# Asking for a weight piece before the factors of unit 0

## The chip, the cores and the metric

One core of one Trainium2 chip runs the kernel. The metric is the device time of one execution in microseconds (us), as the median over several executions. An engine's name stands for its queue of instructions: PE is the matrix engine (TensorE), PEld its weight loads, DVE VectorE, ACT ScalarE, POOL GpSimd, and SP (SyncE) only issues DMAs and waits. ACT issues a few DMAs too.

## What is computed

The reference is a compressed interaction network of three layers over x of shape (512, 39, 32), with 39 fields and 32 embedding columns:

```python
for i in range(3):
    z = einsum('bmd,bnd->bmnd', x, hidden).reshape(B, -1, D)
    cur = relu(einsum('bcd,co->bod', z, Ws[i]) + bs[i][None, :, None])
    # layers 0 and 1: the first 100 of 200 outputs are the next hidden, the rest are kept
    # layer 2: all 200 are kept
result = concatenate(kept, axis=1).sum(axis=-1)      # (512, 400)
```

Everything is float32. Layer 0 has 39 x 39 pairs (780 different ones), layers 1 and 2 have 39 x 100 pairs.

## The kernel before

**Units.** The batch is cut into 4 tiles of 128 rows, and for each tile the 32 columns d are worked one after the other. A pair (tile, d) is a unit, and there are 128 units. For a unit the DVE multiplies two factors into products z (pairs on the partitions, batch rows along the free dimension), ACT rounds z to z_high, DVE makes z_low = z - z_high, and PE multiplies both with weights that are split in the same way (`w_split`, high and low half side by side). That is a float32 product by fast matmuls.

**x by unit.** The factors are rows of x turned round. PE transposes x (`turn_x`, L939), ACT copies the result to SBUF (L770), and `store_x` (L298) writes it with 8 DMAs (L304, L306) to a DRAM tensor `x_by_unit`. From there `load_pairs(u)` (L309) fetches the two factors of layer 0 of unit u, `x_left` and `x_right`, with 6 DMAs over 39 partitions each (L312, L313). `load_xb_rest` (L323) fetches x rows for layers 1 and 2 into the last 32 partitions of `xb`. For units 0 and 1 the other 96 partitions of `xb` are made on PE (L952) and copied by ACT and DVE.

**Weights.** Layer 0's weights fold the two halves of the symmetric pair matrix. They come in by `load_w0` (near part from SP, far part from ACT's queue, both into the memory of z) and are summed on DVE (L587, semaphore `pair_sum`). Layers 1 and 2 have 31 chunks each, loaded in four pieces: `load_w(queue, l, g, ...)` (L251) fetches piece g of layer l into one of two places of a staging area in `mixed` (L260 for 96 partitions, L262 for 32 partitions; a full piece is 600 KB and 200 KB). ACT rounds it into `w_split` (`high_piece`, L774), then DVE writes the low half (`low_piece`, L494). The next piece for the same place waits for that.

**Order.** Each engine has its own program written by hand, and semaphores join them. All places of this case lie in the first 90 us of the program. On SP the order is: load x; copy W0 twice into DRAM (L338, L340); near part of layer 0's weights; `store_x(0)`; wait until all 8 stores have landed (`xt_done`); `load_pairs(0)`; piece 0 of layer 1's weights; wait for the repeats on PE (`repeated`); piece 1; wait for DVE's first product; `load_pairs(1)`; `load_xb_rest` of unit 0; and so on. On DVE: `pair_sum` (L587), `product0` of unit 0 (L514), low half of layer 0's weights, z_low, `low_piece(1, 1, 0)`, `sums`, `low_piece(2, 1, 1)`, `product0` of unit 1, then the first product of layer 1 (L541). On ACT: high half of layer 0's weights, two repeats, z_high, two more repeats, `high_piece(1, 0)`, `second_half` (L731, reads PE's result of unit 0), `dup` (L741), `high_piece(1, 1)`. On PE: repeats, layer 0 of unit 0, a transpose, layer 0 of unit 1, then layers 1 and 0 by turns.

Piece 0 is staged in columns 0 to 1599 of `mixed`; the tile of x that is being turned and stored lies in its last 1280 columns (of 4224), and piece 1 overlaps that.

Of the kernel before, what the change touches and what calls it, by code (L numbers as in the profile page):

```python
# [74 lines left out]
def split_from(layer, g):  # L75
    return WHOLE if (layer, g) == (2, 0) else 0


def split_chunks(layer, g):
    return group_chunks(g) - split_from(layer, g)  # L80
# [23 lines left out]
def cin_kernel(nc, r_x, W0, W1, W2, b0, b1, b2, out):  # L104
# [6 lines left out]
    with ExitStack() as ctx:  # L111
# [90 lines left out]
        def stage(l, g):  # L202
            at, n = g % 2 * STAGED, split_chunks(l, g)
            return mixed[:, at:at + n * O].rearrange("p (c o) -> p c o", o=O)
# [10 lines left out]
        def xts(r):  # L215
            return x_tile(r).rearrange("p (k t) -> p k t", t=T)
# [34 lines left out]
        def load_w(queue, l, g, w, bias):  # L251
            k = GROUPS * (l - 1) + g
            skip, n = split_from(l, g), split_chunks(l, g)
            a = GROUP * g + skip
            wt, row = w.tensor, HID * O
            st = stage(l, g)
            if skip:
                queue.dma_start(w_whole[0:MAIN, :, :], bass.AP(wt, 0, [[O, MAIN], [row, skip], [1, O]])).then_inc(w_whole_in, 16)
                queue.dma_start(w_whole[MAIN:P, :, :], bass.AP(wt, CHUNKS * row, [[O, P - MAIN], [row, skip], [1, O]])).then_inc(w_whole_in, 16)
            queue.dma_start(st[0:MAIN, :, :], bass.AP(wt, a * row, [[O, MAIN], [row, n], [1, O]])).then_inc(w_in[k], 16)  # L260
            if g < GROUPS - 1:
                queue.dma_start(st[MAIN:P, :, :],  # L262
                                bass.AP(wt, (CHUNKS + skip) * row + 32 * g * O, [[O, P - MAIN], [row, n], [1, O]])).then_inc(w_in[k], 16)
            else:
                queue.wait_ge(stage_ready, l)
                full = F // TAIL_CHUNKS
                at = MAIN + TAIL * full
                for t in range(TAIL):
                    queue.dma_start(st[MAIN + t:at:TAIL, 0:TAIL_CHUNKS, :],
                                    bass.AP(wt, (MAIN + t) * O, [[TAIL_CHUNKS * row, full], [row, TAIL_CHUNKS], [1, O]])).then_inc(w_in[k], 16)  # L270
                queue.dma_start(st[at:at + TAIL, 0:F - TAIL_CHUNKS * full, :],
                                bass.AP(wt, TAIL_CHUNKS * full * row + MAIN * O, [[O, TAIL], [row, F - TAIL_CHUNKS * full], [1, O]]))\
                     .then_inc(w_in[k], 16)
                queue.dma_start(st[ONES_ROW:ONES_ROW + 1, 0, :], bass.AP(bias.tensor, 0, [[O, 1], [1, O]])).then_inc(w_in[k], 16)
# [16 lines left out]
        def _(sp):  # L291
# [6 lines left out]
            def store_x(r):  # L298

                sp.wait_ge(xts_in, X_BANKS * (r + 1))  # L300
                at = r * (D * XROWS * T)
                for q in range(Q):
                    part = xts(r)[D * q:D * (q + 1), :, :]
                    sp.dma_start(bass.AP(xt_t, at + q * T, [[XROWS * T, D], [Q * T, BLOCKS], [1, T]]), part).then_inc(xt_done, 16)  # L304
                    k = 1 if q == 0 else 0
                    sp.dma_start(bass.AP(xt_t, at + (F + Q * k + q) * T, [[XROWS * T, D], [Q * T, WRAP_BLOCKS - k], [1, T]]),  # L306
                                 part[:, k:WRAP_BLOCKS, :]).then_inc(xt_done, 16)
# [35 lines left out]
            load_w0(sp, True)  # L343
            sp.dma_start(pair_w[L0_ONES:L0_ROWS, 0, :], bass.AP(b0.tensor, 0, [[O, 1], [1, O]])).then_inc(pairs_w_in, 16)
            store_x(0)
            sp.wait_ge(xt_done, 16 * X_STORES)
            sp.wait_ge(ones_l0, 2)
            load_pairs(0)
            sp.wait_ge(ones_set, 2)
            load_w(sp, 1, 0, W1, b1)  # L350

            sp.wait_ge(repeated, 2 * HALVES * Q)
            load_w(sp, 1, 1, W1, b1)
# [694 lines left out]
```

## Time and profile before

| | us |
|---|---|
| median of 3 executions | 2685.38 |
| lowest, highest | 2685.25, 2686.32 |
| the profiled execution, its time | 2686.64 |
| the profiled execution, its span from first to last instruction | 2684.8 |
| PE busy in the span | 2652.3 (99%) |
| DVE busy | 2633.4 (98%) |
| ACT busy | 1782.6 (66%) |
| DMA, mean over the span | 133 GB/s |

The span is 1.84 us shorter than the time of the same execution; what lies around it is start and end. Times in the trace count from the span's start. Engine queues that only issue carry a q (SPq). In a timeline row the bracket tells how long the engine sat idle before the instruction and what released it. KB are 1024 bytes, MB are 10^6 bytes.

### The profile page before, as it was taken

How to read it: one execution, taken by the hardware profiler on the slowest of the kernel's cores; microseconds unless marked ns; L12 is line 12 of the kernel's file. 1: busy time of each engine (PE TensorE's matmuls, PEld its weight loads, DVE VectorE, ACT ScalarE, POOL GpSimd, SP SyncE). 2: the span in 40 equal slices, each digit the busy share in tenths (PEclk: the TensorE clock that was granted, in tenths of full speed). 3: DMA queues.
4: the chain of work that ended last, by engine and by line, in shares of the span. 5: the costliest groups of instructions: out<-in, count | busy, mean ns of one | idle time of the engine just before them, and what ended most of it. 6: DMA issues, size and time to landing. Idle time of an engine off the chain costs nothing.

```text
span 2684.8 us, 53056 instructions
## 1 busy us (share of the span) xinstructions
PE 2652.3 (99%) x17992; PEld 2639.2 (98%) x17992; DVE 2633.4 (98%) x2593; ACT 1782.6 (66%) x2978; POOL 121.4 (5%) x148
## 2 busy tenths in 40 slices
PE   6999999999999999999999999999999999999999
PEld 4999999999999999999999999999999999999998
DVE  6999999999999999999999999999999999999998
ACT  4666666666666666666666666666666666666665
POOL 0000000000000000000000000000000000000000
PEclk8999999999999999999999999999999999999999
DMA  8555545545565555455456544554555455455542
GB/s 187 138 143 142 132 121 138 141 121 125 143 156 128 129 142 130 120 137 140 125 138 152 140 120 127 143 131 120 135 144 127 124 141 137 120 128 143 129 120 72
DMA packets 249154, 357.76 MB, mean 133 GB/s; under 512 B 30631, under 2 KB 184019, under 8 KB 248959
## 3 DMA queue, kind: packets, MB, share of 16 engines
q1 hardware_dynamic: 229091, 330.02, 47.1%
q0 software_dynamic: 18960, 25.76, 5.5%
q8 instruction: 54, 0.88, 0.1%
q10 hardware_dynamic: 1008, 0.75, 0.1%
q14 instruction: 41, 0.34, 0.0%
HBM read 325.98 MB, written 5.91 MB: 124 GB/s over the span
## 4 chain that ended last, share of the span: by engine, by line
PE 97%; DVE 1%; issue 1%; SPq 1%; DMA 1%; ACT 0%; DVEq 0%
PE acc L917 64%; PE acc L918 30%; PE acc L910 2%; PE turned L930 1%; DVE z_low L547 0%; DMA xb<-x_by_unit 0%; DVE z L541 0%; DMA x_by_unit<-mixed 0%; DMA x_right<-x_by_unit 0%; PE x_turned L939 0%; SPq L338 0%; ACT w_split L774 0%; SPq L340 0%; SPq L312 0%; DVE z L514 0%
## 5 line engine op out<-in xcount | busy, mean ns | idle before, releaser
L917 PE MATMUL acc<-w_split,z_high 128*128 128x400 f32 (+1 forms) x8704 | 2602.7, 367 | 20.4 <-DVE z_low L547 16.4
L918 PE MATMUL acc<-w_split,z_low 128*128 128x200 f32 (+1 forms) x8704 | 2221.8, 255 | 0.0
L726 ACT ACTIVATE z_high<-z 128x1024 fp32r<-128x1024 f32 (+2 forms) x1152 | 1165.7, 1012 | 798.1 <-PE acc L918 497.9
L918 PEld LDWEIGHTS acc<-w_split,z_low 128*128 128x128 f32 (+1 forms) x8704 | 1664.7, 191 | 0.0
L917 PEld LDWEIGHTS acc<-w_split,z_high 128*128 128x128 f32 (+1 forms) x8704 | 1637.3, 188 | 23.6 <-issue 16.1
L547 DVE TENSOR_TENSOR z_low<-z,z_high 128x1024 fp32r<-128x1024 f32 (+2 forms) x1152 | 1336.6, 1160 | 19.1 <-ACT z_high L726 6.9
L541 DVE TENSOR_TENSOR z<-mixed,xb 128x1024 f32<-128x1024 f32 (+1 forms) x1024 | 1213.2, 1185 | 1.1 <-DMA xb<-x_by_unit 0.9
L446 POOL DMA_DIRECT2D direct<-fresh_direct x129 | 113.5, 879 | 2327.6 <-ACT fresh_direct L765 2306.8
L751 ACT ACTIVATE mixed<-turned 32x128 f32<-32x128 f32 x768 | 205.4, 267 | 8.9
L748 ACT ACTIVATE mixed<-turned 96x512 f32<-96x512 f32 x256 | 150.9, 590 | 6.0 <-PE turned L930 1.9
L514 DVE TENSOR_TENSOR z<-x_left,x_right 118x896 f32<-118x896 f32 x128 | 138.6, 1083 | 3.3 <-DMA x_right<-x_by_unit 3.3
L557 DVE TENSOR_TENSOR s<-acc,half 128x400 f32<-128x400 f32 (+1 forms) x130 | 73.0, 562 | 0.7 <-ACT half L731 0.7
L749 ACT ACTIVATE mixed<-turned 32x128 f32<-32x128 f32 x256 | 69.3, 271 | 3.0
L731 ACT ACTIVATE half<-acc 128x400 f32<-128x400 f32 (+1 forms) x130 | 65.0, 500 | 7.6 <-PE acc L918 4.6
L765 ACT ACTIVATE fresh_direct<-s 128x400 f32<-128x400 f32 x126 | 68.0, 539 | 3.1
L910 PE MATMUL acc<-w_whole,z 128*128 128x200 f32 x256 | 66.5, 342 | 0.8 <-DVE s L566 0.8
L741 ACT ACTIVATE s<-s 128x48 f32<-128x48 f32 (+1 forms) x130 | 31.4, 241 | 45.5 <-DVE s L557 45.5
L566 DVE TENSOR_TENSOR s<-acc,half 128x200 f32<-128x200 f32 x128 | 46.0, 360 | 5.7 <-issue 4.0
L930 PE MATMUL turned<-s 128*128 128x128 f32 x256 | 49.3, 273 | 1.1 <-ACT s L741 1.1
L736 ACT ACTIVATE half<-acc 128x200 f32<-128x200 f32 x128 | 40.8, 318 | 7.8 <-PE acc L918 7.8
L910 PEld LDWEIGHTS acc<-w_whole,z 128*128 128x128 f32 x256 | 38.3, 189 | 1.1 <-DVE s L566 1.1
L930 PEld LDWEIGHTS turned<-s 128*128 128x128 f32 x256 | 29.9, 140 | 1.5 <-ACT s L741 1.5
(30 smaller groups left out, 96.7 us busy)
## 6 DMA issues: line engine op xcount, KB each, us to landing
xb<-x_by_unit SPq DMA_DIRECT2D x378, 384.0 KB, 5.2
x_right<-x_by_unit SPq DMA_DIRECT2D x384, 136.5 KB
xb<-x_by_unit SPq DMA_DIRECT2D x384, 128.0 KB, 5.9
xb<-x_by_unit SPq DMA_DIRECT2D x126, 336.0 KB
direct<-fresh_direct POOLq DMA_DIRECT2D x115, 200.0 KB, 7.1
xb<-x_by_unit SPq DMA_DIRECT2D x128, 84.0 KB
x_left<-x_by_unit SPq DMA_DIRECT2D x384, 19.5 KB
mixed<-in_L_rec_W_dram SPq DMA_DIRECT2D x5, 600.0 KB, 6.7
```

What stands on the lines that cost most here:

```text
L446: return pool.dma_start(direct[:, a:b, :].rearrange("p l o -> p (l o)"), fresh_direct[:, a:b, :].rearrange("p l o -> p (l o)"), accum_op=A ...
L514: nc.vector.tensor_tensor(dst, left, x_right[0:L0_ROWS, :, :], ALU.mult).then_inc(product, 1)
L541: nc.vector.tensor_tensor(dst, left, xb[par][:, c0:c0 + n, :], ALU.mult).then_inc(product, 1)
L547: nc.vector.tensor_tensor(z_low[slot % LOW_RING][0:rows, 0:n * T], z[0:rows, z_place(number, slot), 0:n * T], z_high[slot % RING][0:rows, ...
L557: nc.vector.tensor_tensor(s[:, a:b, :, 0:HID], acc[:, a:b, 0:O].rearrange("p l (h o) -> p l h o", o=HID), half[:, a:b, :, :], ALU.add).the ...
L726: nc.scalar.activation(z_high[slot % RING][0:rows, 0:n * T], z[0:rows, z_place(number, slot), 0:n * T], ACT.Copy).then_inc(high, 1)
L748: nc.scalar.activation(h[0:MAIN, :, :], t[0:MAIN, :].unsqueeze(1).to_broadcast([MAIN, GROUPS, T]), ACT.Relu)
L751: last = nc.scalar.activation(h[MAIN:P, g, :], t[32 * g:32 * (g + 1), :], ACT.Relu)
L910: used = nc.tensor.matmul(a[:, 0:O], z_whole[:, c * T:(c + 1) * T], w_whole[:, c, :], start=(c == 0), stop=False, skip_group_check=True)
L917: nc.tensor.matmul(a[:, 0:2 * O], z_high[slot % RING][0:rows, tok], w, start=(c == 0), stop=False, skip_group_check=True)
L918: last = nc.tensor.matmul(a[:, 0:O], z_low[slot % LOW_RING][0:rows, tok], w[:, 0:O], start=False, stop=(c == chunks - 1), skip_group_check ...
L930: last = nc.tensor.transpose(turned[:, 0, l * P:(l + 1) * P], s[:, l, 0, :], ident)
```

## The change

The call that asks for piece 0 of layer 1's weights is moved up on SP: from behind `load_pairs(0)` and the wait for `ones_set` to directly behind `store_x(0)`, ahead of the wait for the stores' landing. The wait for `ones_set` then stands in front of piece 1. Nothing else moves; the other engines' programs are the same.

```diff
             store_x(0)
+            load_w(sp, 1, 0, W1, b1)
             sp.wait_ge(xt_done, 16 * X_STORES)
             sp.wait_ge(ones_l0, 2)
             load_pairs(0)
             sp.wait_ge(ones_set, 2)
-            load_w(sp, 1, 0, W1, b1)
 
             sp.wait_ge(repeated, 2 * HALVES * Q)
             load_w(sp, 1, 1, W1, b1)
```

On SP's queue, from the end of `store_x(0)` (L304, L306) to the first DMA of `load_pairs(1)` (the last row). `mixed<-in_L_rec_W_dram` with 96x8x200 and 32x8x200 is one piece of layer 1's weights; the difference between before (-) and the change (+), with the semaphores waited for:

```order
 L304 DMA x_by_unit<-mixed 32x10x128
 L306 DMA x_by_unit<-mixed 32x5x128
+L260 DMA mixed<-in_L_rec_W_dram 96x8x200
+L262 DMA mixed<-in_L_rec_W_dram 32x8x200
 L312 DMA x_left<-x_by_unit 39x128 [waits ones_l0,xt_done]
 L313 DMA x_right<-x_by_unit 39x7x128
```

The two DMAs of piece 0 now stand between the last store and the wait that `load_pairs(0)` begins with. And where they were:

```order
 L312 DMA x_left<-x_by_unit 39x128
 L313 DMA x_right<-x_by_unit 39x7x128
-L260 DMA mixed<-in_L_rec_W_dram 96x8x200 [waits ones_set]
-L262 DMA mixed<-in_L_rec_W_dram 32x8x200
-L260 DMA mixed<-in_L_rec_W_dram 96x8x200 [waits repeated]
+L260 DMA mixed<-in_L_rec_W_dram 96x8x200 [waits repeated,ones_set]
 L262 DMA mixed<-in_L_rec_W_dram 32x8x200
 L312 DMA x_left<-x_by_unit 39x128 [waits product]
```

Here only piece 1 is left between `load_pairs(0)` and `load_pairs(1)`.

## Rows read from the trace of the kernel before

**Rows 1.** The page: PE's line of busy time, and the chain by engine

```profile
PE 2652.3 (99%) x17992; PEld 2639.2 (98%) x17992; DVE 2633.4 (98%) x2593; ACT 1782.6 (66%) x2978; POOL 121.4 (5%) x148
PE 97%; DVE 1%; issue 1%; SPq 1%; DMA 1%; ACT 0%; DVEq 0%
```

**Rows 2.** Waits of DVE, 20 to 90 us: waited for, us in total, times, longest

```profile
DVE w_split L494 <- ACT w_split L774: 6.0, 5, 2.3
```

**Rows 3.** Waits of PE, 41 to 90 us, same columns

```profile
PE acc L917 <- DVE s L557: 3.2, 1, 3.2
```

**Rows 4.** The chain in order of time, 14 to 42 us: start, us, what

```profile
14.74 4.23 DMA x_by_unit<-mixed
...
21.09 3.62 DMA x_right<-x_by_unit
...
28.75 9.24 DMA xb<-x_by_unit
```

**Rows 5.** Timeline of SP, 14 to 25 us: start, us, engine, line, DMA

```profile
14.74 0.57 SPq L306 DMA_DIRECT2D x_by_unit<-mixed  x1
18.98 0.34 SPq L312 DMA_DIRECT2D x_left<-x_by_unit  x1
...
21.51 0.40 SPq L260 DMA_DIRECT2D mixed<-in_L_rec_W_dram  x1
21.95 0.54 SPq L262 DMA_DIRECT2D mixed<-in_L_rec_W_dram  x1
24.03 0.31 SPq L260 DMA_DIRECT2D mixed<-in_L_rec_W_dram  x1
```

**Rows 6.** Four stretches; the last three columns are PEclk, DMA share, GB/s

```profile
17.25:19.00 1.75, 1.75 (x6) 0.69 (x5) 0.55 (x1) 0.75 (x2) 0.00 (x0) 1.00 0.83 231
19.00:21.00 2.00, 2.00 (x6) 0.71 (x5) 0.87 (x2) 0.78 (x2) 0.00 (x0) 1.00 0.47 99
21.00:23.25 2.25, 2.25 (x7) 0.87 (x6) 1.44 (x1) 1.78 (x3) 0.00 (x0) 1.00 0.68 170
...
25.00:27.00 2.00, 0.00 (x0) 0.00 (x0) 2.00 (x2) 1.00 (x2) 0.00 (x0) 1.00 1.12 239
```

**Rows 7.** The page of 23 to 25 us: GB/s in 40 slices of 0.05 us

```profile
GB/s 143 152 117 80 32 32 64 128 208 192 176 223 196 228 180 244 196 196 228 224 240 208 304 192 272 240 288 208 352 304 304 272 272 208 240 208 240 224 304 256
```

**Rows 8.** DMA queues (q1 SP, q10 ACT), 17.25 to 19, then 19 to 21 us

```profile
q10 hardware_dynamic: 456, 0.34, 70.1%
q1 hardware_dynamic: 141, 0.06, 12.8%
...
q10 hardware_dynamic: 126, 0.09, 28.9%
q1 hardware_dynamic: 227, 0.11, 18.6%
```

**Rows 9.** Timelines of DVE, ACT and PE, 20 to 38 us, by engine

```profile
20.82 1.62 DVE L587 TENSOR_TENSOR z<-z 118x1400 f32<-118x1400 f32 x1 [1.03 <-DMA z<-w_rows_again]
24.82 1.09 DVE L514 TENSOR_TENSOR z<-x_left,x_right 118x896 f32<-118x896 f32 x1 [2.38 <-DMA x_right<-x_by_unit]
...
34.95 1.83 DVE L494 TENSOR_TENSOR w_split<-mixed,w_split 128x1600 fp32r<-128x1600 f32 x1 [1.53 <-ACT w_split L774]
37.66 1.09 DVE L514 TENSOR_TENSOR z<-x_left,x_right 118x896 f32<-118x896 f32 x1 [0.89 <-DMA x_right<-x_by_unit]
...
29.16 1.54 ACT L774 ACTIVATE w_split<-mixed 128x1600 fp32r<-128x1600 f32 x1 [1.34 <-DMA mixed<-in_L_rec_W_dram]
32.44 0.34 ACT L731 ACTIVATE half<-acc 128x200 f32<-128x200 f32 x1 [1.74 <-PE acc L918]
...
33.40 1.52 ACT L774 ACTIVATE w_split<-mixed 128x1600 fp32r<-128x1600 f32 x1
...
28.58 0.42 PE L917 MATMUL acc<-w_split,z_high 118*128 118x400 f32 x1 [4.58 <-DVE z_low L547]
```

**Rows 10.** The microsecond in which PE's first multiplication ends, columns as rows 6

```profile
32.00:33.00 1.00, 0.40 (x2) 0.03 (x1) 0.74 (x2) 0.34 (x1) 0.00 (x0) 0.83 1.10 152
```

## The prediction, made before the change was run

> **What bounds the kernel now.** I read the page first: PE is busy 99% of the span and holds 97% of the chain that ended last [rows 1]. So from about 85 us on the time is PE's own work, the change does not touch it, and all that the change can do is to move the moment at which that work gets going. The waits before it tell who sets that moment. The longest wait of PE for DVE's sums ends at 62.85 us [rows 3], and DVE itself waits in 20 to 90 us mainly for ACT's rounded weights, 6.0 us in five waits [rows 2], and for two landings of `x_right`, 2.38 us and 0.89 us [rows 9]. From 38.7 us on DVE's timeline has no more idle time than three gaps of 0.7 to 0.8 us behind ACT, each of which hangs on work that DVE or PE gave out shortly before. A shift of DVE's start at 37.66 us therefore goes through to the end, one to one. The question is what the change does to the instruction at 37.66 us, `product0` of unit 1.
>
> Three transfers lie in the chain on the way there [rows 4]: the last store of x (4.23 us), `x_right` of unit 0 (3.62 us from its issue at 21.09), and the rest of `xb` (9.24 us from its issue at 28.75, landed at 37.99).
>
> **The change, part by part.**
>
> *Issue on SP.* Two DMAs of piece 0, 0.40 and 0.54 us [rows 5], about 0.95 us with the gaps, now stand behind the last store, whose issue ends at 15.31. SP then waits anyway until 18.98 for the stores' landing, 3.67 us. The 0.95 us are hidden there; if that cover were gone they would cost 0.95 us. `load_pairs(0)` is still issued from 18.98 on. Piece 1 is issued at 24.03 behind the wait for PE's repeats [rows 5]; `load_pairs(0)` was issued by 21.46, so removing 0.95 us behind it moves nothing. The moved wait for `ones_set` costs nothing: DVE's two fills of `xb` are over by 7 us. Piece 0 is requested at 15.35 instead of 21.51, 6.2 us earlier.
>
> *What is released earlier.* ACT waits 1.34 us for piece 0, until 29.16 [rows 9]. Taken alone that wait goes. What is late next? ACT's next step but one, `second_half`, waits for PE's result until 32.44 (1.74 us idle), and the next weights, at 33.40, come only after it [rows 9]. So the 1.34 us are worth nothing to the path: piece 0's low half is on DVE earlier, and PE doesn't need it before 45 us.
>
> *What the DMA queue gains later.* At 37.66 DVE had been idle for 0.89 us behind `low_piece` of piece 1 (34.95, ended 36.77), until `x_right` of unit 1 landed [rows 9]. The following product of layer 1 starts at 38.67, 0.68 us after `xb` landed. Between 25 and 38 us the DMA engines are full (1.12 at 25 to 27 [rows 6]), and most of piece 0, 0.82 MB, stands in that queue ahead of piece 1, the factors of unit 1 and the rest of `xb`. With it gone, 2 to 3 us of this backlog go, and less than one is needed. So `product0` of unit 1 starts at 36.77 instead of 37.66: **0.89 us gained**, and no more, since DVE is busy with `low_piece` up to there.
>
> *What unit 0's factors lose.* This is the term that decides. Piece 0 is now in SP's own DMA queue ahead of the six loads of `load_pairs(0)`. Its bytes take 0.82 MB / 239 GB/s = 3.43 us at the rate of 25 to 27 us, when mostly such weights move [rows 6]. They start about 1.8 us behind the issue: piece 0, issued at 21.51 before, began to move at about 23.3, where the rate climbs again after a dip to 32 GB/s that ends the factors [rows 7]. So now they start at about 17.2, and up to 23.25, where the last bytes of unit 0's factors moved before, they compete with the far part of layer 0's weights (ACT's queue, q10) and the factors. How much room is there? By the share of all 16 engines the idle part is 1.75 x (1 - 0.83) + 2.00 x (1 - 0.47) + 2.25 x (1 - 0.68) = 0.30 + 1.06 + 0.72 = 2.1 us [rows 6]. By that the factors are 3.4 - 2.1 = 1.3 us late. But q10 keeps a share of only 0.70 from 17.25 to 19 although 126 more of its packets are still to come [rows 8], so I read that it uses only about 0.7 to 0.75 of the engines, and these are full: 0.70 / 0.75 + 0.13 is over 1. On them the room is 0 in the first stretch, 2.00 x (1 - 0.289 / 0.75 - 0.186) = 0.86 us in the second, and 0.72 us in the third [rows 6, 8], 1.6 us in all. A transfer lands when its last engine is done, so I take this: 3.43 - 1.58 = **1.9 us late**. The bounds: 0 (the room is used wholly and the packets overlap better than in any stretch shown) and 3.4 us (none of it is used, since the requests stand in a strict order). It can't be below 0: nothing makes the factors of unit 0 earlier.
>
> The Trainium skill (DMA: Bandwidth & Descriptors, "Why a DMA increments its semaphore by 16 and not by 1") has a rule for this: a DMA runs on the largest number of engines, up to 16, that divides its outer dimensions. By it the far weights (24 rows) sit on 12 engines and the factors (39 rows) on 13. The room on the busiest engines would then be some 1.1 us and the factors 2.3 us late, and the sum below would end 0.4 us higher.
>
> *Does the pair sum become the bound?* The far weights landed at 20.8 and their sum ended at 22.44 [rows 9], 2.38 us ahead of the product. Piece 0 shares the engines with them from 17.25 on; even the whole 3.43 us give a landing at 24.2 and an end at 25.9. With the factors landing at 24.8 + 1.9 = 26.7 this stays hidden, and so does ACT's rounding of layer 0's weights (1.4 us), which DVE needs one product later.
>
> *The way from there.* `product0` of unit 0 (24.82) is followed by z_high, z_low, PE's first multiplication at 28.58, `second_half` at 32.44, the sums, and ACT's rounding of piece 1 at 33.40, then DVE's `low_piece` at 34.95 [rows 9]. Each waits for the one before it, so `low_piece` ends 1.9 us later, at 38.7. The same product also releases `load_pairs(1)` and the rest of `xb` on SP, which are issued 1.9 us later: `xb` from 30.7 on. Landing had taken 9.24 us with the queue full; now there are 2 us or more less in it, so it lands by about 37, and DVE needs it at 39.7. PE's clock was at half (1.2 GHz) during that multiplication, after 4.58 us of idleness before it [rows 9], and rose again in 32 to 33 us, where the mean granted was 0.83 [rows 10]. It starts even later now, so it runs at half speed again; if the rise came at the same 32.4 us as before, its last 1.9 us would take half as long, a gain of up to 1 us. I keep this for the range.
>
> **The sum.** +1.9 (factors of unit 0 late) - 0.9 (wait at 37.66 gone) = +1.0 us. On the profiled execution: 2686.64 + 1.0 = 2687.6. The median of the runs, 2685.38, is 1.26 us below that execution, so for a median **2686.4 us**. That is 0.04% slower. A measurement of this kernel can tell about 0.2%, 5.4 us, from no change, so it will count as the same.
>
> **The rivals.**
>
> *A. There is room, and the early request pays.* If piece 0 slips into the idle DMA time before the factors, these are under 0.9 us late and the kernel gets faster, by 0.9 us at the most: 2684.5 to 2685.4. For it: 0.47 share and 99 GB/s at 19 to 21 us [rows 6]. Against it: this dip is short, and piece 0 needs 3.4 us. The Trainium skill (DMA: Bandwidth & Descriptors, "Rules for kernel authors") says for this, in my words, to issue a DMA early and to wait for it late so that its fixed cost is overlapped. Followed as written, it gives this rival.
>
> *B. The factors stand strictly behind the whole piece, and the stores are held up too.* Piece 0 is asked for while stores are still landing (4.23 us for the last [rows 4], in a full DMA). If it takes bandwidth from them, SP is released after 18.98, and with no room used the factors land 3.4 us late and up to 1 us more. Price: +2.5 to +3.5 us, 2687.9 to 2688.9. It decides from the point at which the factors are over 0.9 us late; under that the waits at 37.66 cover it. To get beyond 0.2% they would have to be over 6.3 us late, nearly twice piece 0's whole transfer.
>
> *C. The shift is absorbed.* Between 38 and 85 us something else, such as PE's clock rising earlier or DVE's gaps behind ACT, takes up the microsecond: 2685.1 to 2685.7. PE has idle time there, 3.2 us before 62.85 alone [rows 3], but it isn't the one that is late. DVE is, and it has hardly a gap.
>
> **How the numbers follow.** My forecast (factors 0.9 to 3.0 us late, +0 to +2.1 us) gets 0.60, A 0.17, B 0.13, C 0.10. The range reaches from A's end, 2684.5, to +2.9 or so, 2688.3, and 0.4 us on each side for the scatter of a median whose runs lie 1.07 us apart: 2684.1 to 2688.7. All four lie within 0.2% (2680.0 to 2690.8); 0.01 for faster and 0.02 for slower are for mechanisms that I don't see.
>
> **What would show it.** In the profile after: the weight DMAs at about 15.3 and 15.8 on SP, and `load_pairs(0)` still at about 19.0 (else B). DVE's wait for `x_right` before its first product about 1.9 us longer, that product at 26.7 (A: under 25.7; B: over 28). ACT's wait of 1.34 us for piece 0 gone. DVE's wait at 37.66 gone, with `product0` of unit 1 directly behind `low_piece` at about 38.7. DMA full from 15 to about 25 us and then a dip, until piece 1 starts to move at about 25.8. The span 1 us longer. The prediction would be wrong if the factors land at the old time, if `product0` of unit 1 still waits for a DMA, or if the shift at 38 us isn't the shift at 85 us.

## The result and the profile after

The changed kernel takes 2690.59 us (median of 20 runs, 2689.29 to 2692.12). The kernel before, run 20 times beside it, takes 2686.24 us. The ratio is 1.0015, with a 95% interval of 1.0009 to 1.0021: it is slower by 0.15%, 4.35 us. That is under the 0.2% that I had set as the bound of "the same", but clear of noise, and four times the 1.0 us that I had forecast. The range ended at 2688.7.

The profiled execution took 2690.58 us with a span of 2688.8 us, 4.0 us more than before. Its page begins as before's does [rows 1]:

```profile
PE 2655.2 (99%) x17992; PEld 2642.1 (98%) x17992; DVE 2632.8 (98%) x2593; ACT 1782.2 (66%) x2978; POOL 121.4 (5%) x148
PE 97%; DVE 1%; issue 1%; SPq 1%; DMA 0%; ACT 0%; DVEq 0%; ACTq 0%
```

PE is 2.9 us longer busy at the same number of instructions, so it ran more of them at the lower clock than before. The timeline of SP (start, us, engine, line, DMA), to be read beside [rows 5]:

```profile
14.71 0.48 SPq L306 DMA_DIRECT2D x_by_unit<-mixed  x1
15.24 0.86 SPq L260 DMA_DIRECT2D mixed<-in_L_rec_W_dram  x1
16.14 0.75 SPq L262 DMA_DIRECT2D mixed<-in_L_rec_W_dram  x1
18.65 0.32 SPq L312 DMA_DIRECT2D x_left<-x_by_unit  x1
```

The piece is asked for at 15.24, and the wait for the stores ends at 18.65, no later than before. The rest is told by DVE and ACT, to be read beside [rows 9]:

```profile
26.10 1.62 DVE L587 TENSOR_TENSOR z<-z 118x1400 f32<-118x1400 f32 x1 [5.62 <-DMA z<-w_rows_again]
28.12 1.09 DVE L514 TENSOR_TENSOR z<-x_left,x_right 118x896 f32<-118x896 f32 x1 [0.41 <-DMA x_right<-x_by_unit]
...
38.59 1.83 DVE L494 TENSOR_TENSOR w_split<-mixed,w_split 128x1600 fp32r<-128x1600 f32 x1 [1.53 <-ACT w_split L774]
40.33 1.08 DVE L514 TENSOR_TENSOR z<-x_left,x_right 118x896 f32<-118x896 f32 x1
...
31.19 1.54 ACT L774 ACTIVATE w_split<-mixed 128x1600 fp32r<-128x1600 f32 x1
36.08 0.34 ACT L731 ACTIVATE half<-acc 128x200 f32<-128x200 f32 x1 [3.35 <-PE acc L918]
...
31.92 0.67 PE L917 MATMUL acc<-w_split,z_high 118*128 118x400 f32 x1 [7.23 <-DVE z_low L547]
```

Two things had got late. `product0` of unit 0 starts at 28.12 and not 24.82, 3.3 us later. And the sum of layer 0's weights (L587) starts at 26.10 and not 20.82, 5.3 us later: it ends only 0.4 us ahead of the factors' landing. Both waits that I had expected to vanish have vanished: ACT no longer waits for piece 0 (31.19), and `product0` of unit 1 follows `low_piece` at once (40.33). So the table of shifts reads:

| instruction | before, us | after, us | shift |
|---|---|---|---|
| `product0` of unit 0 on DVE | 24.82 | 28.12 | +3.30 |
| PE's first multiplication | 28.58 | 31.92 | +3.34 |
| `second_half` on ACT | 32.44 | 36.08 | +3.64 |
| `low_piece` of piece 1 on DVE | 34.95 | 38.59 | +3.64 |
| `product0` of unit 1 on DVE | 37.66 | 40.33 | +2.67 |
| last `low_piece` on DVE | 81.70 | 84.31 | +2.61 |
| PE's x transposes of tile 1 (chain) | 133.79 | 136.37 | +2.58 |
| a z_low in the last unit (chain) | 2670.98 | 2673.56 | +2.58 |
| end of the span | 2684.8 | 2688.8 | +4.0 |

Between 134 us and the last unit, a stretch of over 2500 us, not a hundredth of a microsecond is added or lost. The remaining 1.4 us come behind 2673 us. Here are the stretches around PE's last wait, first of the kernel before, then of the changed one (the third number from the right is the granted clock):

```profile
2669.00:2673.00 4.00, 1.65 (x9) 1.18 (x8) 3.43 (x4) 2.23 (x3) 0.00 (x0) 1.00 0.01 4
2673.00:2677.00 4.00, 4.00 (x27) 3.79 (x27) 4.00 (x5) 2.02 (x2) 0.00 (x0) 1.00 0.00 2
```

```profile
2671.00:2675.00 4.00, 1.65 (x10) 1.09 (x9) 2.85 (x4) 2.23 (x3) 0.00 (x0) 1.00 0.02 4
2675.00:2679.00 4.00, 4.00 (x19) 3.98 (x18) 4.00 (x4) 2.01 (x2) 0.00 (x0) 0.59 0.00 2
```

PE is busy for 1.65 us of the first four in both, but in the changed kernel's execution the clock then fell to 1.2 GHz for most of the next four microseconds, and PE got 19 matmuls done and not 27. Whether that belongs to the change is what some of the experiments are for.

### The profile page after: what moved, and what is told of

Read it like the earlier page. It is cut to its first block, busy times and chain, and to the rows that moved or that the text cites. A ratio compares the mean times of both kernels' runs of the same rounds, so it can differ in the third digit from the quotient of the medians.

```text
span 2688.8 us, 53057 instructions
## 1 busy us (share of the span) xinstructions
PE 2655.2 (99%) x17992; PEld 2642.1 (98%) x17992; DVE 2632.8 (98%) x2593; ACT 1782.2 (66%) x2978; POOL 121.4 (5%) x148
## 4 chain that ended last, share of the span: by engine, by line
PE 97%; DVE 1%; issue 1%; SPq 1%; DMA 0%; ACT 0%; DVEq 0%; ACTq 0%
PE acc L917 64%; PE acc L918 30%; PE acc L910 2%; PE turned L930 1%; DVE z_low L547 0%; DVE z L541 0%; DMA x_right<-x_by_unit 0%; DMA x_by_unit<-mixed 0%; PE x_turned L939 0%; DVE z L514 0%; SPq L338 0%; ACT w_split L774 0%; SPq L340 0%; DVE w_split L494 0%; SPq L304 0%
## 5 line engine op out<-in xcount | busy, mean ns | idle before, releaser
L514 DVE TENSOR_TENSOR z<-x_left,x_right 118x896 f32<-118x896 f32 x128 | 138.2, 1079 | 0.4 <-DMA x_right<-x_by_unit 0.4
```

The source lines that it names most:

```text
L514: nc.vector.tensor_tensor(dst, left, x_right[0:L0_ROWS, :, :], ALU.mult).then_inc(product, 1)
```

## The experiments

All the theories here are about three questions: what makes the factors of unit 0 late and why by 3.3 us and not by 1.9; whether PE's clock has a part in the start; and whether the drop of the clock at the end belongs to the change. Ratios are to runs of the kernel before on the same chip; "product0" is the start of L514 of unit 0 on DVE.

**Both kernels a second time** (before_again, after_again).

> The kernel before, unchanged, for a second trace. Theory start (the whole difference is made before 90 us by unit 0's factors being late): product0 of unit 0 starts at 24.8 and DVE's product at 83.2 again, and the last part has no waits that differ. Theory end (1.3 to 1.5 us of the difference come from PE's clock dropping for one step close to the end, by chance of phase): in this second trace the end can show such a drop too, and then its span is about 1.4 us longer than 2684.8 with the same start.

> The changed kernel, unchanged, for a second trace. Both theories: product0 of unit 0 at about 28.1 (3.3 us late), DVE at 85 us shifted by about 2.6 us. Theory start: ratio to before 1.0015 made by that alone, about 4 us, each time. Theory end: the end either shows the 3.4 us drop of the clock again (span 2688.8) or not (span 2687.4).

Before: 2687.18 us (2684.99 to 2688.39, 11 runs), ratio 1.0 (0.9991 to 1.0009), product0 at 25.19, span 2686.6. Changed: 2690.27 us (2688.63 to 2692.17, 11 runs), ratio 1.0011 (1.0002 to 1.002), product0 at 28.03, span 2688.9. The lateness of the factors and of the weight sum repeats:

```profile
25.33 1.62 DVE L587 TENSOR_TENSOR z<-z 118x1400 f32<-118x1400 f32 x1 [4.75 <-DMA z<-w_rows_again]
28.03 1.09 DVE L514 TENSOR_TENSOR z<-x_left,x_right 118x896 f32<-118x896 f32 x1 [1.08 <-DMA x_right<-x_by_unit]
```

The rest varies. In the second trace of before, DVE waited 0.66 us at `product0` of unit 1 (38.11), and its last `low_piece` came at 83.08, 1.4 us later than in the first trace. The shift of that instruction is 2.6 us between the first two traces and only 0.7 us between the second two (83.76 in the changed kernel). A single pair of traces does not give the shift to a microsecond. The drop of the clock at the end is there again in the changed kernel and again not in the kernel before.

**Less of the piece, and more** (small_early, more_early). First only the part for 32 partitions is asked for early, and the part for 96 at the old place:

```diff
             store_x(0)
-            load_w(sp, 1, 0, W1, b1)
+            load_w(sp, 1, 0, W1, b1, "small")
...
             sp.wait_ge(ones_set, 2)
+            load_w(sp, 1, 0, W1, b1, "large")
```

> Only the 32-partition part of piece 0 (200 KB of 800) is asked for ahead of the factors, the 600 KB part stays at the old place. Theory order (the factors are late by the time that the bytes ahead of them in SP's queue take): factors 0.8 us late, a quarter of 3.3, product0 of unit 0 at 25.6, wait at 37.66 partly gone, total about that of before. Rival room (there is idle DMA time at 19 to 21 us that takes a small request): factors 0 to 0.3 us late, product0 of unit 0 at 24.8 to 25.1.

```profile
22.78 1.62 DVE L591 TENSOR_TENSOR z<-z 118x1400 f32<-118x1400 f32 x1 [2.93 <-DMA z<-w_rows_again]
25.53 1.09 DVE L518 TENSOR_TENSOR z<-x_left,x_right 118x896 f32<-118x896 f32 x1 [1.14 <-DMA x_right<-x_by_unit]
```

(Lines of this kernel are 4 higher.) product0 at 25.53, 0.7 us later than in the mean of three traces of before, 24.85 (24.82, 25.19 and, below, 24.53). 2688.16 us (11 runs), ratio 1.0006 (0.9997 to 1.0015), so the total is not told from before's. That looks as if even 200 KB, which need 0.9 us of the DMA, found no room. But SP's timeline tells where the 0.7 us arose:

```profile
19.75 0.34 SPq L315 DMA_DIRECT2D x_left<-x_by_unit  x1
```

The stores released SP at 19.75, and not at 18.98, 19.03 and 18.74 as in those three traces. From there product0 followed after 5.78 us, against 5.84, 6.16 and 5.79. So behind the release the 200 KB cost nothing; the 0.7 us are the later landing of the last store. Whether the 200 KB held that store up isn't shown: in four traces with the whole 800 KB at this place the release came at 17.91 to 19.03.

Then the whole piece and 600 KB more (DVE and ACT also get a wait for the extra loads before they use those tiles, not shown):

```diff
             load_w(sp, 1, 0, W1, b1)
+            for i, spare in enumerate((fresh_direct[:, :, :].rearrange("p l o -> p (l o)"), direct[:, :, :].rearrange("p l o -> p (l o)"),
+                                      half[:, :, :, :].rearrange("p l h o -> p (l h o)"))):
+                sp.dma_start(spare.rearrange("p (c o) -> p c o", o=O),
+                             bass.AP(W1.tensor, 2 * i * HID * O, [[O, P], [HID * O, 2], [1, O]])).then_inc(extra_in, 16)
```

> The changed kernel with three more loads of W1 rows (600 KB in the same 800-byte rows, into tiles that are overwritten later) directly behind piece 0, so 1400 KB stand ahead of the factors and not 800. Theory price per byte (every 200 KB ahead of the factors makes them 0.8 to 0.9 us later, no idle DMA time is used): product0 of unit 0 at 30.4 to 31.0, the total 2.5 us over the changed kernel, at 2692.5 to 2693.5, and 0.25% over the kernel before. Rival fixed (the 3.3 us come mainly from the meeting of piece 0 with the stores and the far weights, not from its size): product0 of unit 0 under 29.5 and the total within 1 us of the changed kernel.

```profile
25.73 1.62 DVE L592 TENSOR_TENSOR z<-z 118x1400 f32<-118x1400 f32 x1 [5.21 <-DMA z<-w_rows_again]
30.82 1.09 DVE L519 TENSOR_TENSOR z<-x_left,x_right 118x896 f32<-118x896 f32 x1 [3.48 <-DMA x_right<-x_by_unit]
```

product0 at 30.82, as expected; 2693.9 us (10 runs), a little over the expected 2692.5 to 2693.5, ratio 1.0023 (1.0014 to 1.0032). With 0, 200, 800 and 1400 KB ahead of the factors product0 starts at 24.85, 25.53, 28.19 (the mean of 28.12, 28.03 and, below, 28.47 and 28.14) and 30.82 us. That is 0.7, 3.3 and 6.0 us. From 800 to 1400 KB it is 2.6 us, 0.88 us for each 200 KB, and over the first 800 KB it comes to 0.84 us for each. So in sum the price goes by the bytes, and the rival of a fixed price falls. The step to 200 KB is no proof that the first bytes are paid too, since its 0.7 us came from the release. The time followed with +1.5, +4 and +6.9 us against the runs of before beside it (the +1.5 is within the noise).

**Another queue for the piece** (act_queue).

```diff
             sp.wait_ge(ones_set, 2)
-            load_w(sp, 1, 0, W1, b1)
...
             load_w0(act, False)
+            load_w(act, 1, 0, W1, b1)
```

> Piece 0 is asked for on ACT's DMA queue, behind the far part of layer 0's weights, from about 17 us on, and not on SP's. Theory order (what hurts is that the factors stand behind it in the same queue): the far weights land as before (20.8), the factors share the engines and are 1 to 2 us late, product0 of unit 0 at 26 to 27. Rival bytes (only the amount of data counts, whichever queue): factors about 3.3 us late, at 28.1, as in the changed kernel. ACT issues about 1 us longer, which may make the repeats on PE 1 us later.

product0 at 29.45, weight sum at 22.97, 2691.21 us (11 runs), ratio 1.0016 (1.0007 to 1.0025). The factors were issued on SP from 18.52 on, and the piece on ACT's queue from 17.22 to 18.42. The DMA queues in 19 to 21, in 21 to 23, and in 23 to 25 us (packets, MB, share of 16 engines):

```profile
q10 hardware_dynamic: 371, 0.28, 111.2%
...
q10 hardware_dynamic: 477, 0.37, 113.2%
...
q10 hardware_dynamic: 442, 0.34, 80.8%
q1 hardware_dynamic: 109, 0.05, 13.4%
```

In four microseconds the factors' queue moved nothing, although its requests had been made. They were served when ACT's queue had nearly finished. So it isn't the order within SP's queue that hurts. What was asked for first went first here, although on another queue, and the factors paid for all of it. (In the changed kernel, where the piece and the far weights were asked for at nearly the same time, the two queues did move together: shares of 62.8% and 36.9% in 17 to 19 us.) The theory of the queue's order falls here, and the rival of the bytes is confirmed (28.1 expected, 29.45 measured; the DMAs ran at only 140 GB/s in 19 to 21, which may be the rest). The Trainium skill (DMA: Bandwidth & Descriptors, "Queues, rings and completion order") says that an engine takes turns between the queues that have work. By that the factors would have moved from about 20.3 on; this trace doesn't agree. Whether the factors' requests had reached the engines by then, it doesn't show.

**Behind the stores, ahead of the factors** (behind_wait).

```diff
             sp.wait_ge(ones_l0, 2)
+            load_w(sp, 1, 0, W1, b1)
             load_pairs(0)
```

> Piece 0 is asked for behind the wait for the stores and directly ahead of the factors: in the order of SP's queue it is where the change puts it, but it can't meet the stores or most of the far weights. Theory order: the pair sum starts at 20.8 as before, the factors wait for 0.95 us of issue and for all of the transfer that no longer finds room, product0 of unit 0 at 27.9 to 28.5. Rival mix (the excess over my 1.9 us comes from piece 0 and the far weights slowing each other): product0 of unit 0 clearly earlier than in the changed kernel, at 26 to 27.

```profile
22.20 1.62 DVE L587 TENSOR_TENSOR z<-z 118x1400 f32<-118x1400 f32 x1 [1.42 <-DMA z<-w_rows_again]
28.67 1.09 DVE L514 TENSOR_TENSOR z<-x_left,x_right 118x896 f32<-118x896 f32 x1 [4.85 <-DMA x_right<-x_by_unit]
```

product0 at 28.67, weight sum at 22.20; 2690.77 us (10 runs), ratio 1.0017 (1.0008 to 1.0026). Here the piece met hardly any far weights, and the sum was nearly on time. The factors were as late as in the changed kernel, 0.95 us of it by the issue. That refutes the rival's 26 to 27: the factors are late by this much without the mixing of piece 0 with the far weights. It doesn't show that the mixing costs nothing in the changed kernel, since here the piece is also asked for 3.5 us later (18.76 and not 15.24) and misses the DMA time ahead of 19 us. The 4 us appear again in the total. The late weight sum of the changed kernel is therefore a second delay that lies beside the first and adds nothing to it.

**Without the far weights** (no_far_before, no_far_after). In both kernels `load_w0(act, False)` and its part of the wait are left out, so layer 0's weights are incomplete.

> The kernel before without the loads of the far part of layer 0's weights (and without the wait for them), so layer 0's result is not the reference's. Control for the next run: product0 of unit 0 stays at 24.8, or up to 0.5 us earlier, since the factors are then bound by their issue on SP.

> The changed kernel without the loads of the far part of layer 0's weights. Theory mix: with no far weights on the engines piece 0 runs from 17.2 to about 20.7 in time that is then idle, and the factors are 0 to 0.6 us late against the control. Theory order alone: they stand behind piece 0 all the same and are over 2 us late against the control.

One run each: 2686.01 and 2685.82 us. In the first, product0 starts at 22.64 directly behind the weight sum (20.89), without a wait for the factors; SP was released by the stores at 17.42 in both. In the second it waits 2.95 us for the factors, until 24.26. So the factors are at least 1.6 us later. The trace's packets of 512 bytes on SP's queue, which from the stores' landing on are the factors', tell more: their last ended at 21.7 us in the first and at 23.6 us in the second, 1.9 us later, where the whole piece is worth 3.4 us. That was neither the 0 to 0.6 us of one theory nor the over 2 us of the other: where the DMA stands idle ahead of the factors, part of the piece fits in. The control has another lesson: without the far weights the stores release SP 1.3 to 1.6 us earlier than in the three traces of before. The totals are alike, since the first kernel waits for other things (1.01 us for ACT's rounding).

The factors' own transfer differs between the two. DMA queue of SP in 19 to 21 us of the control and in 21 to 23 us of the other, both almost only factors:

```profile
q1 hardware_dynamic: 718, 0.34, 59.0%
```

```profile
q1 hardware_dynamic: 748, 0.35, 91.8%
```

The same 0.34 to 0.35 MB in two microseconds, once at a share of 59% and once at 92%. In the first they are moved as SP issues them, in the second they all stand ready, and on average they go no faster. So a share of busy time is no measure of the bytes that still fit. In 21 to 23.25 us of before [rows 6], at a share of 68%, the factors moved at 170 GB/s, and 171 and 176 GB/s are what they reach here. That other bytes would have found no time between them is argued from this and not run.

**PE kept busy close to the end** (tail_busy_before, tail_busy_after). Six extra 128x128 matmuls into an unused bank in PE's last waits; `dummies(n)` issues n of them.

```diff
             at = first(UNITS)
+            dummies(2)
             pe.wait_ge(s2_in, UNITS - 1)
             for g in range(GROUPS):
-                multiply(2, at + g, at + g, g)
+                multiply(2, at + g, at + g, g, 4 if g == 0 else 0)
...
                     used.then_inc(whole_used, 1)
+                    dummies(filler)
```

> The kernel before with 6 extra matmuls on PE (into an unused bank, 0.27 us each) in PE's waits close to the end, at about 2669 and 2670.6 us. Theory end: no drop of the clock in the last 20 us of any run, runs scatter less, median as before or up to 1 us lower. Theory start: nothing changes but noise; if the extra matmuls outlast the waits, up to 0.5 us more.

> The changed kernel with the same 6 extra matmuls close to the end. Theory end: the drop of the clock at 2675 us is gone, the span falls by about 1.4 us to about 2687.4, and against the kernel before with the same filling the difference is 2.6 us. Theory start: the difference stays at 4 us.

Before: 2685.61 us (11 runs, 2683.96 to 2686.56), ratio 0.9995 (0.9986 to 1.0004), product0 at 24.53, span 2683.8. Changed: 2689.73 us (11 runs), ratio 1.0011 (1.0002 to 1.002), product0 at 28.47, span 2688.2. The clock stays up now; the stretches of the former:

```profile
2668.00:2671.00 3.00, 2.04 (x15) 1.66 (x14) 2.51 (x4) 2.10 (x3) 0.00 (x0) 1.00 0.02 5
2671.00:2674.00 3.00, 2.96 (x19) 2.76 (x19) 3.00 (x3) 1.20 (x2) 0.00 (x0) 1.00 0.00 0
2674.00:2677.00 3.00, 3.00 (x23) 3.00 (x22) 2.81 (x4) 0.95 (x1) 0.00 (x0) 1.00 0.01 3
```

Both medians fall by about as much, though neither clear of noise: by 1.15 us from 2686.76 for the kernel before, and by 0.5 to 0.9 us for the changed one (against 2690.27 and 2690.59). The difference between them stays: 2689.73 - 2685.61 = 4.1 us, and 4.4 us between the two spans. So the drop at the end has no visible share in the change's price. Other traces bear this out: those of behind_wait and act_queue, whose medians lie 4.0 and 4.5 us over the runs of before beside them, show no drop while PE works off its last units, and that of no_far_before, which has the order of the kernel before, has one (mean granted clock 0.75 in 2668 to 2672 us). Theory end falls as an explanation of the difference, and my reading of the first pair (2.6 us from the start, 1.4 from the end) does not hold for the medians: in the filled pair the last `low_piece` on DVE starts at 80.64 and 84.72, all 4.1 us of the difference ahead of 85 us.

**PE kept busy at the start** (start_busy_before, start_busy_after). Extra matmuls between PE's last repeat and its first multiplication, so that it is computed at the full clock: 15 in the kernel before, 26 in the changed one.

```diff
+            dummies(15)
             pe.wait_ge(w_low_done, 1)
             multiply(0, 0, 0)
```

> The kernel before with 15 extra matmuls on PE between its last repeat (24.0 us) and its first multiplication (28.6 us), so that the clock stays up. The multiplication takes 2 us and not 3.8. Theory DMA: DVE's low_piece of piece 1 ends 1.5 to 2 us earlier, but product0 of unit 1 still waits for the DMA until about 37.6, so the total gains 0 to 0.5 us.

> The changed kernel with 26 extra matmuls from 24.7 us on. Here the backlog in the DMA is gone, so the path from the factors through PE's multiplication is all that counts: the multiplication takes 2 us and not 3.9, and product0 of unit 1 starts at about 38.4 and not 40.3. Total 1.9 us under the changed kernel, about 2 us over the kernel before. If the multiplication isn't on the path, nothing changes.

```profile
31.91 0.42 PE L917 MATMUL acc<-w_split,z_high 118*128 118x400 f32 x1 [0.92 <-DVE z_low L547]
...
34.22 0.34 ACT L731 ACTIVATE half<-acc 128x200 f32<-128x200 f32 x1 [1.66 <-PE acc L918]
...
38.48 1.08 DVE L514 TENSOR_TENSOR z<-x_left,x_right 118x896 f32<-118x896 f32 x1
```

Changed kernel: PE starts at 31.91 as before, `second_half` follows at 34.22 and not at 36.08, and `product0` of unit 1 at 38.48 (38.4 expected). 2688.6 us (11 runs), ratio 1.0006 (0.9997 to 1.0015), 1.7 to 2.0 us under the changed kernel. So the multiplication at half clock is on the path, as I had it. Kernel before: 2684.87 us median, 1.8 us under the 2686.71 beside it, but in two heaps: six runs at 2684.2 to 2684.9 with a mean granted clock of 0.997, five at 2687.4 to 2688.8 with 0.996; ratio 1.0 (0.9991 to 1.0009). In its trace `product0` of unit 1 starts at 35.24 right behind `low_piece` (33.50), without any wait for the DMA. I had expected the DMA to hold it until 37.6. In the third trace of the kernel before, the one with only the end filled, it doesn't wait either (36.37 behind 34.63). So the wait at 37.66, which I had counted as a gain of 0.89 us, is there in two traces with the kernel's own start (0.89, 0.66) and missing in the third, and in this one.

**Both fillings on the kernel before** (both_busy_before), the only version to which this points as faster:

> The kernel before with both sets of extra matmuls, 15 ahead of PE's first multiplication and 6 close to the end. If the two effects of the clock are independent: 1.1 us (end) and on average 0.5 us (start) under the kernel before, 2685.1, less than a measurement can tell from it with 0.2%.

2685.34 us (11 runs, 2684.17 to 2687.35), ratio 0.9993 (0.9984 to 1.0002). It is the likely best of all, by 1.7 us in the medians, but the interval holds 1.

## Why the prediction was wrong

By its own steps:

- *What bounds the kernel.* Right. Everything is decided before 85 us, and from 134 us to the last unit the shift stays at 2.58 us to the hundredth.
- *Issue on SP, what is released earlier.* Right in the changed kernel. The 1.6 us of issue (0.86 and 0.75, longer than 0.40 and 0.54 before) were hidden behind the stores, SP was released at 17.9 to 19.0, and ACT's vanished wait of 1.34 us brought nothing.
- *What unit 0's factors lose.* This is the step that failed. I subtracted 1.6 us of "room" from the 3.4 us of transfer, which left 1.9 us. The factors were 3.3 us late, close to the upper bound of 3.4 that I had written beside it. more_early confirms the size: 600 KB more cost 2.6 us more. The error was to read an idle DMA share as time in which bytes move at 239 GB/s. The changed kernel's stretches, to be read beside [rows 6], tell where it lies:

```profile
17.25:19.00 1.75, 1.75 (x6) 0.79 (x5) 0.56 (x2) 0.66 (x2) 0.00 (x0) 1.00 1.02 274
19.00:21.00 2.00, 2.00 (x6) 0.78 (x5) 0.69 (x1) 0.88 (x2) 0.00 (x0) 1.00 1.05 222
21.00:23.25 2.25, 2.25 (x7) 0.85 (x6) 0.00 (x0) 1.43 (x3) 0.00 (x0) 1.00 0.91 185
23.25:25.00 1.75, 1.44 (x4) 0.33 (x2) 0.00 (x0) 0.00 (x0) 0.00 (x0) 1.00 0.93 160
25.00:27.00 2.00, 0.00 (x0) 0.00 (x0) 0.90 (x1) 0.00 (x0) 0.00 (x0) 0.99 0.99 191
```

  Up to 23.25 us they moved 1.34 MB, against 0.98 MB before. So 0.36 MB of the piece's 0.82 MB did fit in, about what 1.6 us at 239 GB/s are (0.38 MB). But the other 0.46 MB of the backlog, by then far weights and factors, moved at 160 and 191 GB/s and not at 239, though the share was over 0.9. That takes 2.7 us instead of 1.9. What is left of the 3.3 us stays open; piece 1, asked for at 24.77, then moves beside the last factors. The pair of controls shows the same from the other side: the factors moved 0.34 MB in 2 us at a share of 59% and 0.35 MB at 92%. The rule of the Trainium skill on the number of engines, which I had weighed beside it, pointed the right way but gave 2.3 us and not 3.3.
- *Does the pair sum become the bound?* Said to end by 25.9 at the latest; it ended at 27.7. The far weights of ACT's queue had to share the engines with piece 0 (23.5% and 81.6% in 19 to 21 us). It is only 0.4 us short of being the bound, so with the factors on time `product0` would still have been 2.9 us late by it (argued from the trace; behind_wait shows only the reverse, a sum nearly on time and late factors).
- *What the DMA queue gains later.* The wait vanished, but it was worth 0.89 us only in the trace I had read. Over three traces with the same start (0.89, 0.66, 0) it is 0.5 us.
- *The way from there.* The chain was right, link by link. PE's first multiplication took 0.3 us longer (32.44 - 28.58 = 3.86 against 4.16), since its first 0.4 us were no longer at the full clock; the gain of up to 1 us, kept for the range, didn't come. start_busy_after gained its 1.9 us exactly there.

With the measured sizes the sum is 3.3 + 0.3 - 0.5 = 3.1 us at 40 us. The medians of the two kernels differ by 4.35 us in the first comparison and by 3.6 us in the second (3.1 us, if only the eleven runs of before_again are taken). What stays open is up to a microsecond between the two. Three traces of each kernel give the last `low_piece` at 81.70, 83.08, 80.64 against 84.31, 83.76, 84.72: 2.45 us on average, from 0.7 to 4.1 by pairs. PE's clock also fell and rose at other moments in each of them (in 33 to 34 us it was 1.00 in the first trace of before and 0.50 in the second), and I did not separate what that is worth.

Of the rivals, A (there is room) is refuted. B came nearest: it had the right price for the factors, but in the changed kernel's traces the stores were not held up, and it gave them as the reason for the rest. C (absorbed) is refuted by 136 to 2673 us. The range failed at its upper end for two reasons. It allowed +2.9 us and 0.4 for scatter, with no term for the clock, though the rows showed PE at half speed on the path (it cost 0.3 us more). And it stood on a median of three runs, 2685.38; the median of twenty is 2686.24, so 0.9 us of the 4.2 between forecast and result (2686.4, 2690.59) lie in the base.

## What to carry to other kernels

Before moving a prefetch ahead of a load that is waited for, price it at its full transfer time. An idle DMA share in front of the urgent load is not worth its time: here 0.36 MB more did move in it, and the load was still late by nearly the whole transfer, since what was left moved at 160 to 191 GB/s and not at the 239 of the sum. Where the DMA stood wholly idle ahead of the load, as without the far weights, 1.5 of the 3.4 us were saved (one trace of each). Moving the request to another issuing queue did not help: there too the factors waited until nearly all of the earlier request had been served. And a gain that rests on one wait of under a microsecond should be looked for in a second trace before it enters a sum.

## What was not expected of the hardware

- With the piece on ACT's queue, SP's queue moved no packet from 19 to 23 us, although its DMAs were issued from 18.52 on; ACT's held 111 and 113% of the engines in that time, the first half of it at only 140 GB/s.
- With 1400 KB asked for ahead, SP's own issue became slow: two of the three small `x_left` DMAs took 1.53 and 2.30 us to issue, against 0.41 us. Timeline of SP in more_early:

```profile
18.79 0.34 SPq L313 DMA_DIRECT2D x_left<-x_by_unit  x1
19.17 0.37 SPq L314 DMA_DIRECT2D x_right<-x_by_unit  x1
19.59 1.53 SPq L313 DMA_DIRECT2D x_left<-x_by_unit  x1
21.16 0.38 SPq L314 DMA_DIRECT2D x_right<-x_by_unit  x1
21.58 2.30 SPq L313 DMA_DIRECT2D x_left<-x_by_unit  x1
```

- PE's clock fell to 1.2 GHz after 1.65 us of work in 4 us in an execution of the changed kernel and not after as much in one of the kernel before, and cost 1.4 us there.
